# Scan step of a four-layer vision network: half 1's product written over B's row in PSUM and scanned there in one piece

## The reference

```python
dt = softplus(einsum('bkrl,kdr->bkdl', dts, dt_projs_w) + dt_projs_b)
def step(h, t):
    dt_t, u_t, B_t, C_t = t
    h = h * jnp.exp(dt_t[..., None] * A) + (dt_t * u_t)[..., None] * B_t[:, :, None, :]
    y = jnp.einsum('bkdn,bkn->bkd', h, C_t)
    return (h, y)
_, ys = jax.lax.scan(step, h0, ts)
```

## Time and profile before

| | |
|---|---|
| median of three runs | 30018.37 us (30010.79 to 30018.79) |
| the profiled execution | 30034.11 us |
| its span | 30032.1 us |
| mean granted TensorE clock | 0.846 |
| busy: TensorE / VectorE / ScalarE / GpSimd | 76% / 76% / 41% / 73% |
| idle time of GpSimd with no other releaser than its own issue | 6395.7 us over 21168 gathers |
| idle time of VectorE for B's row (L1324) | 1601.3 us, 698 times |

### The profile page before, as it was taken

One profiled execution on the slowest core, in us unless ns is written; L12 is line 12 of the kernel. 1 busy time (PEld: TensorE's weight loads), 2 busy tenths in 40 slices (PEclk: granted clock), 3 DMA queues, 4 the chain that ended last, 5 costly groups with the idle time before them and its releaser, 6 DMA issues.

```text
span 30032.1 us, 287320 instructions
## 1 busy us (share of the span) xinstructions
PE 22752.8 (76%) x94224; PEld 14355.0 (48%) x94224; DVE 22824.8 (76%) x36140; ACT 12178.8 (41%) x21705; POOL 21870.4 (73%) x21172
## 2 busy tenths in 40 slices
PE   5588788787887888877887788777877787777444
PEld 4444455444554454444544454445544454445433
DVE  1289987989599868998788859997799968994212
ACT  1144444444444444444444435444444444443000
POOL 6777777777677777777677767776677767566767
PEclk7798889888888888888988888888888888888666
DMA  3212222221222222212222122212222222112221
GB/s 76 74 54 68 55 68 68 61 65 52 75 63 56 64 74 54 66 52 62 70 62 66 49 73 59 61 54 66 60 59 64 55 71 55 46 49 70 63 58 53
DMA packets 2410663, 1854.55 MB, mean 62 GB/s; under 512 B 1686547, under 2 KB 2045509, under 8 KB 2409165
## 3 DMA queue, kind: packets, MB, share of 16 engines
q0 software_dynamic: 677376, 1388.62, 17.3%
q1 hardware_dynamic: 1731788, 447.55, 6.7%
HBM read 1569.35 MB, written 265.21 MB: 61 GB/s over the span
## 4 chain that ended last, share of the span: by engine, by line
DVE 35%; PE 29%; POOL 14%; issue 12%; ACT 7%; DMA 1%; SPq 1%; DVEq 0%; ACTq 0%; POOLq 0%
POOL d_g L746 14%; DVE l_wk L1334 7%; DVE l_wk L1311 7%; PE d_p L1037 6%; PE l_acc L1019 5%; DVE l_wk L1328 5%; DVE d_g L1354 5%; PE d_pr L1185 3%; DVE l_wk L1313 2%; PE d_pr L1239 2%; ACT l_pm L797 2%; PE d_pr L1072 1%; PE d_pr L1051 1%; ACT L973 1%; PE d_pr L1232 1%
## 5 line engine op out<-in xcount | busy, mean ns | idle before, releaser
L746 POOL DMA_INDIRECT d_g<-table,d_idx x21168 | 21870.2, 1033 | 8119.0 <-issue 6395.7
L1037 PE MATMUL d_p<-d_g,c_ident 128*128 128x128 f32 x43200 | 6019.1, 303 | 2046.9 <-DVE d_g L1354 2043.0
L1019 PE MATMUL l_acc<-l_wk,c_ident 128*128 128x448 f32 x14336 | 7290.6, 638 | 331.5 <-DVE l_yx L1299 263.7
L1037 PEld LDWEIGHTS d_p<-d_g,c_ident 128*128 128x128 f32 x43200 | 5874.6, 218 | 3118.9 <-DVE d_g L1354 2149.0
L1324 DVE TENSOR_TENSOR l_wk<-l_wk,l_pb 128x896 f32<-128x896 f32 x3584 | 3814.9, 1064 | 1604.7 <-PE l_pb L988 1601.3
L797 ACT ACTIVATE l_pm<-l_wk,l_a 128x448 f32<-128x448 f32 x3584 | 2271.2, 634 | 6232.1 <-DVE l_wk L1311 6219.5
L1019 PEld LDWEIGHTS l_acc<-l_wk,c_ident 128*128 128x128 f32 x14336 | 3174.7, 223 | 2397.9 <-issue 2224.1
L1334 DVE TENSOR_TENSOR l_wk<-l_wk,l_pc 128x896 f32<-128x896 f32 x3584 | 3795.0, 1059 | 38.0 <-ACT l_carry L778 24.2
L1311 DVE TENSOR_TENSOR_SCAN l_wk<-l_pm,l_carry,l_wk 128x448 f32<-128x448 f32 x3072 | 3496.9, 1138 | 5.1 <-ACT l_pm L797 2.3
L1354 DVE TENSOR_TENSOR d_g<-d_g,d_wt 128x512 f32<-128x512 f32 x1281 | 812.6, 688 | 2291.6 <-DMA d_g<-table,d_idx 2291.3
L1328 DVE TENSOR_TENSOR_SCAN l_wk<-l_wk 128x224 f32<-128x224 f32 x3584 | 2421.3, 676 | 0.3
(11 more groups left out here) (180 smaller groups left out, 23765.5 us busy)
## 6 DMA issues: line engine op xcount, KB each, us to landing
d_g<-table,d_idx POOLq DMA_INDIRECT x21168
table<-d_pst SPq DMA_DIRECT2D x2376, 64.0 KB
hd<-d_hst SPq DMA_DIRECT2D x168, 224.0 KB
d_htc<-hd SPq DMA_DIRECT2D x144, 256.0 KB
d_xin<-mid SPq DMA_DIRECT2D x112, 224.0 KB
mid<-d_xo SPq DMA_DIRECT2D x192, 128.0 KB
d_xres<-mid SPq DMA_DIRECT2D x192, 128.0 KB
d_xin<-in_x SPq DMA_DIRECT2D x56, 224.0 KB
```

Source lines behind the costliest of these rows:

```text
L746: e.indirect_dma_start(out=m.g[Q % SLOTS][:, j, :], out_offset=None, in_=m.table[k % 2], in_offset=bass.IndirectOffsetOnAxis(ap=m.idx[G % ...
L1019: ins = e.matmul(m.acc[:, h, 0:448], m.ident[:, :], m.hb[x % 4][:, h, :], start=(n == 0), stop=(n == 15))
L1037: ins = e.matmul(m.p0[:, t % 2 * 128:t % 2 * 128 + 32 * w], m.ident[:, :], m.g[Q % SLOTS][:, w * p:w * p + w, 32 * r:32 * r + 32], start=( ...
```

## The change

The item `"sB"` goes; B's row of step S+1 is now written by TensorE at the end of `"s"`, behind the accumulation. VectorE makes dt*u*B of step S inside step S itself, in two products of 448: half 0 into `hb`, half 1 over the row of B in its PSUM bank. It then scans half 1 in one piece with the product read from PSUM, which frees B's bank, then half 0, and then multiplies by C. Three semaphores change with it: `f_pb` now tells of the scan of half 1, `sh` counts scans of half 0 alone, and the scans wait for their own products (`bm1`, `bm0`). ScalarE's conditions follow.

```diff
@@ vss_ticks
-            tick = [("sB", i, sig - 1)] * (0 <= sig < NSTEP) + [("s", i, sig)]
+            tick = [("s", i, sig)]
@@ scalar_program
-                e.wait_ge(s["sh"], 2 * S)
+                e.wait_ge(s["sh"], S)
+                e.wait_ge(s["f_pb"], J.free("B", S - 1))
                 e.activation(m.carry[:, :, n], m.hb[(S - 1) % 4][:, :, end], ACT.Copy).then_inc(s["ca"], 1)
...
                 if h == 0 and x:
-                    e.wait_ge(s["sh"], 2 * x - 1)
+                    e.wait_ge(s["sh"], x)
                 if h == 1 and x >= 3:
-                    e.wait_ge(s["sh"], 2 * x - 4)
+                    e.wait_ge(s["f_pb"], J.free("B", x - 3))
@@ tensor_program
                 ins.then_inc(s["accd"], 1)
-        elif kind == "sB":
-            _, i, sig = item
-            if sig + 2 < NSTEP:
-                row_of_B(NSTEP * i + sig + 2)
+            if sig + 1 < NSTEP:
+                row_of_B(S + 1)
@@ vector_program
-                e.wait_ge(s["f_pb"], J.free("B", S))
-                e.wait_ge(s["dA0"], S + 1)
-                e.tensor_tensor_scan(hb[:, 0, way], m.dA0[:, way], hb[:, 0, way], ini[0], ALU.mult, ALU.add).then_inc(s["sh"], 1)
-                e.wait_ge(s["dA1"], S + 1)
-                e.tensor_tensor_scan(hb[:, 1, one], dA1[:, one], hb[:, 1, one], ini[1], ALU.mult, ALU.add).then_inc(s["s1h"], 1)
...
-                e.tensor_tensor(m.hb[x % 4][:, :, :], m.dtu[P % 2][:, :, :], bc(m.pb[:, 0:448], 1, 2),
-                                ALU.mult).then_inc(s["f_pb"], 1)
-            if 0 <= sig < NSTEP:
-                e.wait_ge(s["s1h"], S + 1)
-                e.tensor_tensor_scan(hb[:, 1, two], dA1[:, two], hb[:, 1, two], hb[:, 1, mid:mid + 1],
-                                     ALU.mult, ALU.add).then_inc(s["sh"], 1)
+                e.wait_ge(s["p_pb"], J.full("B", S))
+                e.tensor_tensor(hb[:, 0, :], m.dtu[P % 2][:, 0, :], row, ALU.mult).then_inc(s["bm0"], 1)
+                e.tensor_tensor(row, m.dtu[P % 2][:, 1, :], row, ALU.mult).then_inc(s["bm1"], 1)
+                e.wait_ge(s["bm1"], S + 1)
+                e.wait_ge(s["dA1"], S + 1)
+                e.tensor_tensor_scan(hb[:, 1, way], dA1[:, way], row[:, way], ini[1], ALU.mult, ALU.add).then_inc(s["f_pb"], 1)
+                e.wait_ge(s["bm0"], S + 1)
+                e.wait_ge(s["dA0"], S + 1)
+                e.tensor_tensor_scan(hb[:, 0, way], m.dA0[:, way], hb[:, 0, way], ini[0], ALU.mult, ALU.add).then_inc(s["sh"], 1)
```

More of the change, by code:

```diff
@@ L369, in bank_uses @@
         s = NSTEP * i + sig
[L370 to L373, removed]
-        _, i, sig = item
-        return [("pb", ("B", NSTEP * i + sig + 2))] if sig + 2 < NSTEP else []
+        uses = [("pc", ("C", s - 1))] if 1 <= sig <= NSTEP else []
+        return uses + [("pb", ("B", s + 1))] if sig + 1 < NSTEP else uses
     if kind == "g":
@@ L1003, in tensor_program @@
             S = NSTEP * i + sig
-            if sig == -1:
-                row_of_B(S + 1)
             if 1 <= sig <= NSTEP:
@@ L1304, in vector_program @@
                 ini = [0.0 if c == (6 if kd >= 2 else 0) else m.carry[:, h, n:n + 1] for h in range(2)]
-                way, one, two, mid = slice(None), slice(0, 224), slice(224, 448), 223
-                if kd >= 2:
-                    way, one, two, mid = slice(None, None, -1), slice(447, 223, -1), slice(223, None, -1), 224
-                e.wait_ge(s["f_pb"], J.free("B", S))
-                e.wait_ge(s["dA0"], S + 1)
-                e.tensor_tensor_scan(hb[:, 0, way], m.dA0[:, way], hb[:, 0, way], ini[0], ALU.mult, ALU.add).then_inc(s["sh"], 1)
-                e.wait_ge(s["dA1"], S + 1)
-                e.tensor_tensor_scan(hb[:, 1, one], dA1[:, one], hb[:, 1, one], ini[1], ALU.mult, ALU.add).then_inc(s["s1h"], 1)
-            if sig + 1 < NSTEP:
-                x = S + 1
-                P, n = divmod(x, 16)
+                way = slice(None, None, -1) if kd >= 2 else slice(None)
+                row = m.pb[:, 0:448]
+                P = S // 16
                 if n == 0:
                     e.wait_ge(s["d2"], P + 1)
-                if sig == -1:
+                if sig == 0:
                     e.wait_ge(s["p_pc"], J.full("pi2", 7 * i + 6))
@@ L1322, in vector_program @@
                         e.wait_ge(s[f"xn{b}"], v_)
-                e.wait_ge(s["p_pb"], J.full("B", x))
-                e.tensor_tensor(m.hb[x % 4][:, :, :], m.dtu[P % 2][:, :, :], bc(m.pb[:, 0:448], 1, 2),
-                                ALU.mult).then_inc(s["f_pb"], 1)
-            if 0 <= sig < NSTEP:
-                e.wait_ge(s["s1h"], S + 1)
-                e.tensor_tensor_scan(hb[:, 1, two], dA1[:, two], hb[:, 1, two], hb[:, 1, mid:mid + 1],
-                                     ALU.mult, ALU.add).then_inc(s["sh"], 1)
+                e.wait_ge(s["p_pb"], J.full("B", S))
[7 more added lines that the diff above has]
+                e.tensor_tensor_scan(hb[:, 0, way], m.dA0[:, way], hb[:, 0, way], ini[0], ALU.mult, ALU.add).then_inc(s["sh"], 1)
             if 1 <= sig <= NSTEP:
@@ L1623 @@
          "weighed accq ysa ytp yta idx wtr w0 pv py exd bst agg sqd x1r xor gbr dgr bsq bnr "
-         "wps dA0 dA1 s1h sh ca accd d1 d2 hd0 md m2 lo ab ex uu qq s1 ln pag psq xir brd lag lsq xmr gsq gt gb tg").split()
+         "wps dA0 dA1 bm0 bm1 sh ca accd d1 d2 hd0 md m2 lo ab ex uu qq s1 ln pag psq xir brd lag lsq xmr gsq gt gb tg").split()
 def program(nc, a, out, n_img=8, layers=(0, 1, 2, 3)):
```

## The result

The changed kernel takes 30530.07 us (median; 30515.51 to 30551.97), the kernel before 30014.83 beside it: ratio 1.0172, 95% interval 1.0155 to 1.0190. It is slower by 0.52 ms. The profiled execution took 30522.55 us with a span of 30520.6, 488.5 more than before.

What follows compares the result with a forecast made beforehand. VectorE and TensorE, each in order and waiting for the other in turn, were taken to pace the scan. VectorE's +0.36 and row waits' +0.15 ms, +0.51 on the 30018 us median, gave 30520 us; range 29400 to 31400.

Steps and rivals of the forecast that it cites:

- Own work: VectorE's scan step: two products, one longer scan and a wait add 0.10 us a step, +0.36 ms over 3584 steps.
- the wait for the own product: VectorE before half 1's scan: it needs the product right before it and starts 0.09 us after its end, +0.17 us.
- TensorE: VectorE's waits for rows: +0.08 us a step from TensorE's smaller freedom, -0.04 against it, together +0.15 ms.
- VectorE's wait for C's row 1.5 ms or more: Sign that the forecast is right: this wait appears in place of the wait for B's row.
- ScalarE at nothing: ScalarE's dA0, waiting for half 0's later scan, priced at nothing; its other late work kept within the bounds given.
- TensorE's wait for ScalarE named in the prediction: TensorE's waits for ScalarE in the same tick, 538 us at L1239, start later; no more than the bounds.
- GpSimd: Gathers within half 1's scan gain up to 0.36 us, at most 1.2 ms of GpSimd's time; 0 in the sum.
- The rival that GpSimd sets the pace: Shorter gathers within half 1's scans shorten the scan by up to 1.2 ms: 29200 us, chance 0.05.
- The rival that rows come in time: C's row, needed 1.66 us later, absorbs lateness; 60% of 1575 us of waits go: 29430 us, chance 0.21.
- The heavier rival: TensorE loses 0.45 us in most ticks, VectorE waits for C's row: +0.36 + 0.8 to 1.6 ms, 31200 us, chance 0.16.
- the freedom of TensorE as a price: How far TensorE may lag: 3.1 us before, 2.6 after; VectorE's row waits grow by about the sixth to fifth lost.

Runs made afterwards that it cites:

- the two variants without that wait: Half 0's scan put ahead of half 1's, in the changed kernel (30744.88 us) and in its variant with half 1's product in SBUF (30112.19 us).
- half 0 first: Changed kernel with half 0's scan ahead of half 1's, so B's row comes free 1.06 us later: 30744.88 us, ratio to the kernel before 1.0233.
- B's row late: Kernel before with only B's row on TensorE moved behind the accumulation: 32377.28 us, ratio 1.0777.

## Why the prediction was right

The time, 30520 predicted and 30530 measured, is the sum of two terms, and the account gives both.

- *Own work*, +0.10 us a step, +0.36 ms. Measured: busy +225 and hole +127, 0.35 ms. Its parts were less exact: the two products take 0.53 each, not 0.51; the wait for the own product costs 0.12 us (0.65 against 0.53), not 0.17; the scans are at 1.07 and 1.04, taken as 1.06. The errors nearly cancel, which is luck. The Trainium skill (VectorE: DVE Perf Modes, section "The DRAIN you can't avoid") prices a semaphore behind each instruction at nothing. For an instruction that waits for the one right before it this case measures otherwise: the two variants without that wait are 0.45 ms shorter in own work than their counterparts with it.
- *TensorE*, +0.15 ms. Measured: rows and carry +196, with +0.14 ms for all waits but the hole. The 0.15 was the difference of two rough guesses, +0.08 and -0.04 us a step, so that it came this close is in part luck. The place was right: the wait moved from B's row to C's (1232 us), and TensorE stands 2106 us before B's row. "VectorE's wait for C's row 1.5 ms or more" was a little high; C's row and carry make 1.53 together.
- *ScalarE at nothing*. Its waits for half 0's scan grew from 6028 to 9729 us, and VectorE's wait for the carry from 23 to 301, which the prediction hadn't seen. The experiment with the carry copied early shows that the 301 cost nothing of their own. Of the later dA0 VectorE shows no wait (0.0 us before L1316); for the copy of weights it waits 41 us in the stretch instead of 7, and TensorE's wait for ScalarE named in the prediction grew from 538 to 602. These are within the bounds given, and no variant tried them alone.
- *GpSimd*: at most 1.2 ms of relief, none of it in the time. Measured 1.2 ms, and waits for a free buffer up by 1.5 ms. That the size fits is luck: gathers begun within scans of half 1 gave 0.74 ms (3681 of them, 0.20 us each, not 0.36), and most of the rest came from gathers that the prediction didn't count. The rival that GpSimd sets the pace was wrong for this kernel; at 0.45 ms less own work, with the product in SBUF, waits for gathers begin to show.
- The rival that rows come in time failed for the reason given against it: TensorE starts the rest of its tick later. The heavier rival asked for 0.8 to 1.6 ms of waits; that size was reached only in variants in which a row came later still (+0.86 ms with half 0 first, +2.3 with B's row late).
- *The step that didn't carry far* is the freedom of TensorE as a price. It gave the right sign each time (freer with the row freed early: -0.15 ms; tighter with half 0 first: +0.66), but a growth in proportion to the loss is good only near where it was read. In the late-row variant it gave 1.1 ms where 2.35 were measured.

Why the waits for rows rise by just this amount was argued, from one tick and from the variants on both sides, and not derived tick by tick. One part of it the prediction left out: TensorE's sums, which now stand right behind its wait for B's row, last 319 ns a record instead of 303 (over 43200 records), while the accumulation, which has less waiting ahead of it (616 us before C's row instead of 1174), lasts 615 instead of 638. What that does to the waits isn't separated.

## What to carry to other kernels

When two in-order engines pace each other, put down for each the own time from start to start and the waits, and ask of every moved instruction when it frees what the other engine needs next: filling a hole of 0.12 us took 0.45 ms from VectorE's own work, and freeing a row 1.06 us later put 0.66 ms on its waits. Relief for an engine that isn't waited for bought nothing here, 1.2 ms of it, and turned into waits for buffers; it can come to count once the pacing engine is made faster. An instruction that waits for the one directly before it should have another between them, unless that delays somebody else.

## What the runs showed of the hardware

- The next instruction of VectorE starts 0.08 us before the one ahead ends, or 0.03 us after it if it waits for it. A product that is written to PSUM lasts 620 ns against 612 for the same one written to SBUF, so writing there cost nothing that counts.
- A scan reading its second input from PSUM instead of SBUF takes as long (1147 and 1152 ns in the two forms). It is the second SBUF input that slows gathers begun within it: 1250 ns on average with it, 944 without. Gathers begun while a product with one SBUF input is written to SBUF take 944 as well.
- Where TensorE stands matters for the work right behind. With 3325 us of waits ahead of C's row, before the accumulation, a record of the accumulation lasted 693 ns and one of the sums 307; with 3630 us ahead of B's row, before the sums, they lasted 604 and 331; in the kernel before 638 and 303. The granted clocks of the three runs are 0.817, 0.834 and 0.846.
